# Score products of three groups in one run, sums of one or two key tiles behind them, in an attention and expert kernel

## The reference

```python
q = (layernorm(x) @ Wq.T).reshape(B, L, H, D) * D ** -0.5
k = (ctx @ Wk.T).reshape(B, -1, H, D)
v = (ctx @ Wv.T).reshape(B, -1, H, D)
scores = sigmoid(einsum('blhd,bshd->bhls', q, k))
x = x + einsum('bhls,bshd->blhd', scores, v).reshape(B, L, E) @ Wo.T
h = layernorm(x)
# 16 experts take 64 tokens of each batch by softmax gate, and one shared
# expert takes all: gelu(h Wg) * (h Wu) Wd, added to x
```

## Time and profile before

| | us |
|---|---|
| median of 3 runs | 1501.34 |
| lowest and highest | 1501.15, 1503.25 |
| the profiled execution's own time | 1503.28 |
| its span | 1501.4 |
| TensorE busy | 1412.4 (94%) |
| ScalarE busy | 888.2 (59%) |
| VectorE busy | 698.8 (47%) |
| weighted sums on TensorE, L1170, 3328 matmuls | 447.8 |
| scores on TensorE, L1154, 1664 matmuls | 316.8 |
| sigmoids on ScalarE, L608, 832 | 780.8 |

### The profile page before, as it was taken

The page is one execution under the profiler, slowest core; times in us unless marked ns, Lnnn a source line. Parts: engine busy times, 40 slices in busy tenths (PEclk is TensorE's granted clock), DMA queues, the critical chain, the costliest instruction groups (busy, mean ns, idle before and its releaser), DMA issues.

```text
span 1501.4 us, 22519 instructions
## 1 busy us (share of the span) xinstructions
PE 1412.4 (94%) x9046; PEld 786.8 (52%) x9046; DVE 698.8 (47%) x1369; ACT 888.2 (59%) x965; POOL 315.2 (21%) x203
## 2 busy tenths in 40 slices
PE   3888999999999999999999999998999999999996
PEld 2433344434434434444443443325888887778775
DVE  4334234225325314423522531224578987767764
ACT  0475877787787787788878779993211222222220
POOL 0000000000000000000000000020001588888885
PEclk9898999999999999999999999998999999999998
DMA  4573485396287467458639528613443545555543
GB/s 154 168 124 103 109 134 147 109 139 166 97 128 144 134 105 128 144 109 130 152 109 155 135 78 109 136 53 127 140 136 104 182 96 137 137 137 133 135 97 42
DMA packets 101144, 187.73 MB, mean 125 GB/s; under 512 B 17200, under 2 KB 51504, under 8 KB 101040
## 3 DMA queue, kind: packets, MB, share of 16 engines
q1 hardware_dynamic: 84192, 155.06, 44.2%
q0 software_dynamic: 16000, 29.91, 10.6%
q10 hardware_dynamic: 848, 1.31, 0.3%
HBM read 122.24 MB, written 64.00 MB: 124 GB/s over the span
## 4 chain that ended last, share of the span: by engine, by line
PE 76%; POOL 9%; DVE 5%; DMA 4%; issue 3%; ACT 2%; SPq 1%; POOLq 0%; DVEq 0%
PE acc L1170 25%; PE score L1154 17%; PE score L1210 11%; PE misc L1068 6%; PE misc L1081 6%; PE score L1225 4%; POOL gu_lo L532 3%; POOL out L564 3%; POOL d_lo L532 2%; PE misc L1104 2%; PE misc L1089 2%; ACT probs L608 2%; DMA key_scr<-key_parts 1%; PE misc L1113 1%; PE misc L1096 1%
## 5 line engine op out<-in xcount | busy, mean ns | idle before, releaser
L608 ACT ACTIVATE probs<-score 128x1024 f32<-128x1024 f32 (+1 forms) x832 | 780.8, 1048 | 205.8 <-PE score L1154 205.0
L1170 PE MATMUL acc<-probs,values 128*32 128x512 f32 (+1 forms) x3328 | 447.8, 610 | 5.7 <-ACT probs L608 3.1
L1154 PE MATMUL score<-queries,keys 48*128 48x512 f32 (+1 forms) x1664 | 316.8, 454 | 2.7 <-DMA keys<-key_scr 2.7
L617 ACT ACTIVATE gelu<-score 128x512 f32<-128x512 f32 x96 | 57.5, 599 | 346.3 <-PE score L1210 344.1
L1154 PEld LDWEIGHTS score<-queries,keys 48*128 48x128 f32 (+1 forms) x1664 | 127.3, 182 | 255.6 <-ACT probs L608 204.4
L510 POOL DMA_DIRECT2D ctx_raw<-ctx_t x32 | 23.4, 733 | 808.4 <-DVE ctx_lo L682 807.3
L1170 PEld LDWEIGHTS acc<-probs,values 128*32 128x32 f32 (+1 forms) x3328 | 66.4, 108 | 153.0 <-issue 131.4
L688 DVE CAST key_parts<-misc 128x512 fp32r<-128x512 f32 (+1 forms) x64 | 36.8, 576 | 213.2 <-PE misc L1068 198.7
L1210 PE MATMUL score<-tok_hi,gu_hi 128*128 128x512 f32 x384 | 121.4, 398 | 7.9 <-POOL gu_lo L532 7.9
L1210 PE MATMUL score<-tok_lo,gu_hi 128*128 128x512 f32 x384 | 119.7, 393 | 0.0
L1210 PE MATMUL score<-tok_hi,gu_lo 128*128 128x512 f32 x384 | 119.3, 392 | 0.0
(11 more groups left out here) (126 smaller groups left out, 1518.6 us busy)
## 6 DMA issues: line engine op xcount, KB each, us to landing
keys<-key_scr SPq DMA_DIRECT2D x180, 200.2 KB, 10.3
key_scr<-key_parts SPq DMA_DIRECT2D x48, 512.0 KB, 4.4
gu_raw<-w_gu SPq DMA_DIRECT2D x17, 1024.0 KB, 5.6
ctx_raw<-ctx_t POOLq DMA_DIRECT2D x24, 512.0 KB, 4.4
queries<-query_scr SPq DMA_DIRECT2D x180, 64.0 KB, 3.0
d_raw<-w_d SPq DMA_DIRECT2D x17, 512.0 KB, 6.7
query_scr<-query_parts SPq DMA_DIRECT2D x15, 512.0 KB, 2.9
xn<-x SPq DMA_DIRECT2D x8, 512.0 KB, 3.8
```

Source lines behind the costliest of these rows:

```text
L608: act.activation(probs[0:rows, n % RING, 2 * pair:2 * pair + 2, :], score[k % 3][0:rows, :, :], ACT.Sigmoid, scale=SCALE).then_inc(probs_d ...
L1154: mm = pe.matmul(score[k % 3][0:rows, g, :], keys[quarter % KEY_RING][of, pair, P * st:P * st + rows], queries[half][of, e, pair, :], star ...
L1170: mm = pe.matmul(acc[32 * c:32 * (c + 1), :], values[b % 2][0:rows, st, half, c, :], probs[0:rows, n % RING, c, :], start=(st == 0), stop= ...
```

## The change

The order on TensorE is no longer made by quads but by cycles, in a list (`PLAN`) that all engines follow. Cycle c begins with the scores of three groups, 3c to 3c + 2, that is one and a half quads. Then come the weighted sums of the quads both of whose groups are in earlier cycles and that are not summed yet: one quad in odd cycles, two in even ones. Then come the tasks whose quad (by the same table, `beside`) falls in the cycle. Where a cycle has two tasks, the first stands ahead of the sums; where a quarter ends in the cycle, the task stands behind that quarter's last sum. VectorE's and SyncE's steps follow the same plan. The arithmetic, the tiles, the three score tensors and the room for three quads in `probs` stay.

The diff, with SyncE's and VectorE's loops cut (they call the same steps as before, by cycle in place of quad):

```diff
@@ -24,12 +24,13 @@
 SCALE = HD ** -0.5
 
 
+
 QUARTERS = 4 * B
 QPB = 4 * NST
 QUADS = QPB * B
 GROUPS = 2 * NST
 RING = 3
-LAG = 2
+RUN = 3
 KEY_RING = 3
 
 
@@ -95,7 +96,31 @@
 
 
 BESIDE = [beside(b) for b in range(B)]
-ORDER = BEFORE + [BESIDE[b][q] for b in range(B) for q in sorted(BESIDE[b])]
+
+
+def cycle_of(b, q):
+    return 2 * (QPB * b + q) // RUN
+
+
+def quads_summed(c):
+
+    return range((RUN * c - RUN) // 2 if c else 0, min(QUADS, RUN * c // 2))
+
+
+
+PLAN = []
+for c in range(cycle_of(B, 0) + 2):
+    sums = [("S", n) for n in quads_summed(c)]
+    tasks = [BESIDE[b][q] for b in range(B) for q in sorted(BESIDE[b]) if cycle_of(b, q) == c]
+    last = [i for i, (_, n) in enumerate(sums) if n % NST == NST - 1]
+    if len(tasks) > 1:
+        steps = tasks[:1] + sums + tasks[1:]
+    elif last:
+        steps = sums[:last[0] + 1] + tasks + sums[last[0] + 1:]
+    else:
+        steps = sums + tasks
+    PLAN.append(steps)
+ORDER = BEFORE + [step for steps in PLAN for step in steps if step[0] != "S"]
 AFTER = [("O", B - 1, 0), ("O", B - 1, 1), ("N", B - 1, 0), ("N", B - 1, 1), ("G", B - 1)]
 ORDER += AFTER
 
...
@@ -405,38 +430,37 @@
                     write_keys(task)
             load_resid_a(0)
             load_x(1)
-            for b in range(B):
-                for q in range(QPB):
-                    if q == 0 and b:
+            for c, steps in enumerate(PLAN):
+                for b in range(1, B):
+                    if c == cycle_of(b, 0):
                         stack_queries(b, 1)
                         stack_keys(4 * b + 2)
-                    if q == NST and b:
+                    if c == cycle_of(b, NST):
                         stack_keys(4 * b + 3)
-                    task = BESIDE[b].get(q)
-                    if task is not None:
-                        if task[:3] == ("K", 0, 0):
-                            first_keys(task[3])
-                        elif task[0] == "K":
-                            write_keys(task)
-                        elif task[0] == "Q":
-                            write_queries(*task[1:])
-                            if task == ("Q", 0, 1):
-                                stack_queries(0, 1)
-                                stack_keys(2)
-                                stack_keys(3)
-                            elif task[2] == 0:
-                                stack_queries(task[1], 0)
-                        elif task[0] == "T" and task[2] == KC - 1 and task[1] + 1 < B:
-                            load_x(task[1] + 1)
-                        elif task == ("N", b - 1, 0):
-                            store_norm(b - 1)
-                        elif task == ("N", b - 1, 1):
-                            store_norm_t(b - 1)
-                        elif task == ("G", b - 1):
-                            load_resid_a(b)
-                        if task == ("K", b + 1, 1, NCH - 1):
-                            stack_keys(4 * b + 4)
-                            stack_keys(4 * b + 5)
+                for task in steps:
...
@@ -836,32 +860,32 @@
...
+            for c, steps in enumerate(PLAN):
+                for step in steps:
+                    if step[0] != "S":
+                        copy_out(step)
+                    elif step[1] % NST == NST - 1:
+                        acc_out(step[1] // NST)
...
@@ -1137,24 +1161,24 @@
                     mm = gate_product()
                 mm.then_inc(misc_full, 1)
 
-            def scores(n):
+            def scores(k):
+                n, pair = divmod(k, 2)
                 b, half, e, st = quad_of(n)
                 quarter, rows = n // NST, key_rows(st)
-                if quarter == 0 and st % (CHUNK // P) == 0:
-                    pe.wait_ge(first_keys_in[P * st // CHUNK], STACK_DMAS)
-                if quarter and st == 0:
-                    pe.wait_ge(keys_in[quarter % KEY_RING], keys_loaded(quarter))
-                if e == 0 and st == 0:
-                    pe.wait_ge(queries_in[half], 2 * STACK_DMAS * (b + 1))
-                for pair in range(2):
-                    k = 2 * n + pair
-                    wait_past(pe, probs_done, k - 2)
-                    for g in range(2):
-                        of = slice(ROWS * g, ROWS * g + STACK)
-                        mm = pe.matmul(score[k % 3][0:rows, g, :],
-                                       keys[quarter % KEY_RING][of, pair, P * st:P * st + rows],
-                                       queries[half][of, e, pair, :], start=True, stop=True)
-                    mm.then_inc(scores_done, 1)
+                if pair == 0:
+                    if quarter == 0 and st % (CHUNK // P) == 0:
+                        pe.wait_ge(first_keys_in[P * st // CHUNK], STACK_DMAS)
+                    if quarter and st == 0:
+                        pe.wait_ge(keys_in[quarter % KEY_RING], keys_loaded(quarter))
+                    if e == 0 and st == 0:
+                        pe.wait_ge(queries_in[half], 2 * STACK_DMAS * (b + 1))
+                wait_past(pe, probs_done, k - 2)
+                for g in range(2):
+                    of = slice(ROWS * g, ROWS * g + STACK)
+                    mm = pe.matmul(score[k % 3][0:rows, g, :],
+                                   keys[quarter % KEY_RING][of, pair, P * st:P * st + rows],
+                                   queries[half][of, e, pair, :], start=True, stop=True)
+                mm.then_inc(scores_done, 1)
 
             def weighted_sum(n):
                 b, half, e, st = quad_of(n)
@@ -1182,18 +1206,17 @@
             pe.wait_ge(w_split, 6)
             for task in BEFORE[4:]:
                 product(task)
-            for n in range(QUADS):
-                b, q = divmod(n, QPB)
-                scores(n)
-                if n >= LAG:
-                    weighted_sum(n - LAG)
-                if n == QPB:
+            for c, steps in enumerate(PLAN):
+                for k in range(RUN * c, min(RUN * c + RUN, 2 * QUADS)):
+                    scores(k)
+                if c == cycle_of(1, 0):
                     pe.wait_ge(w_split, 8)
                     pe.wait_ge(gate_split, 2)
-                if q in BESIDE[b]:
-                    product(BESIDE[b][q])
-            for n in range(QUADS - LAG, QUADS):
-                weighted_sum(n)
+                for step in steps:
+                    if step[0] == "S":
+                        weighted_sum(step[1])
+                    else:
+                        product(step)
             product(AFTER[0])
             product(AFTER[1])
```

More of the change, by code:

```diff
@@ new lines, in _ @@
+                for task in steps:
+                    if task[:3] == ("K", 0, 0):
+                        first_keys(task[3])
+                    elif task[0] == "K":
+                        write_keys(task)
+                        if task[2:] == (1, NCH - 1) and task[1]:
+                            stack_keys(4 * task[1])
+                            stack_keys(4 * task[1] + 1)
+                    elif task[0] == "Q":
+                        write_queries(*task[1:])
+                        if task == ("Q", 0, 1):
+                            stack_queries(0, 1)
+                            stack_keys(2)
+                            stack_keys(3)
+                        elif task[2] == 0:
+                            stack_queries(task[1], 0)
+                    elif task[0] == "T" and task[2] == KC - 1 and task[1] + 1 < B:
+                        load_x(task[1] + 1)
+                    elif task[0] == "N" and task[2] == 0:
+                        store_norm(task[1])
+                    elif task[0] == "N":
+                        store_norm_t(task[1])
+                    elif task[0] == "G":
+                        load_resid_a(task[1] + 1)
@@ L837, in _ @@
                 copy_out(task)
[L839 to L842, removed]
-                    if q in BESIDE[b]:
[L844 to L852, removed]
+            for c, steps in enumerate(PLAN):
[4 more added lines that the diff above has]
+                        acc_out(step[1] // NST)
+                if c == cycle_of(0, 11):
+                    split_weight(WO)
+                    dve.wait_ge(gate_in, 16)
+                    dve.tensor_copy(gate_hi[:], gate_raw[:]).then_inc(gate_split, 1)
+                    dve.wait_ge(gate_split, 1)
+                    dve.tensor_tensor(gate_lo[:], gate_raw[:], gate_hi[:].bitcast(F32), ALU.subtract
+                                      ).then_inc(gate_split, 1)
+                for b in range(B):
+                    if b and c == cycle_of(b, 7):
@@ L853, in _ @@
                         second_sums(b - 1)
-                    if b and q == 9:
+                    if b and c == cycle_of(b, 9):
                         norm_scale()
-                    if b and q == 11:
+                    if b and c == cycle_of(b, 11):
                         norm_apply(norm, resid, norm_ready)
-                    if b + 1 < B and q == (21 if b == 0 else 15):
```

(6 more changed lines are left out.)

## The result

The changed kernel takes 1557.26 us (median of 4 runs, 1554.38 to 1563.84) against 1502.3 (4 runs): a ratio of 1.0372, 95% interval 1.0337 to 1.0406. It is slower by 55 us, where 32 were forecast. In the text, a low-clock window is a stretch in which the granted clock is 0.50, 1.2 GHz instead of 2.4; in these traces it lasts 3.4 us or a multiple of that.

The account below looks back on a forecast made before the run. TensorE bounds batches 0 to 6, ScalarE batch 7. Middle batches +3.8 each (+23 for six), batch 0 +5, batch 7 +4: +32 us on the 1501.34 median, 1533 predicted; 8-in-10 range 1514 to 1554.

Parts of the forecast that it names:

- The sign: Whole kernel: the change makes it slower, chance 0.87; faster 0.09, same 0.04.
- the mechanism: Attention scores: with three banks, a run's third group waits for the previous run's third sigmoid, so nothing carries between cycles.
- rival D: Vector engine's norm work meets shorter gaps, idle TensorE may bring lower clock: 10 to 25 us more, 1543 to 1558; chance 0.20.
- What a longer run saves: TensorE: 0.10 us saved per run of three, 0.14 per second sum in a row; together 5.6 us a batch.
- Rival A: Score runs: the third group costs 0.335 as the second does, not 0.235; +12 us, 1545; chance 0.12.
- The stall: After empty one-sum cycles the third score group waits for ScalarE: 1.09 us each, 56 times in batches 1 to 6.
- so only 2.2 of 122.0 are waits: Middle batches before the change: 2.2 us of each batch's 122.0 are waits, subtracted because the new count replaces them.
- The vector engine: After a chunk's last V product, the copy and context split delay the next K product: 0.8 us, four times in six batches.
- Other copies fit in 1.90: VectorE's copies other than the context-split chain finish within 1.90 us, so they add no cost.
- Batch 7: ScalarE is the bound; a pair of cycles takes 5.75 against 5.49 us, 17 pairs x 0.25, +4 us.
- Batch 0: First batch: 7 stalls x 1.09 + 1.3 - 5.6 + 2 for keys, +5 us.
- The keys of batch 1: Last key product comes 11 groups ahead of first use, not 12; about 1 to 2 us more wait, once.

Follow-up runs that it names:

- pull: Changed kernel, where an odd one-sum cycle has no product and the next has, that product moved one cycle earlier; 1507.39 us, ratio 1.0018 to the kernel before.
- late: Changed kernel with the third score group, in cycles following an empty one-sum cycle, moved behind the first sum; 1533.49 us, ratio 1.0190 to the kernel before.
- half_after: Changed kernel with sigmoids over half of each head's columns (256 of 512), the rest of probs zero; 1475.34 us, ratio 0.9799 to the kernel before.
- quads7: Changed kernel with the old order, scores of one quad then one sum, from quad 366 on (batch 7); 1555.49 us, ratio 1.0317 to the kernel before.
- norm: Changed kernel with the vector engine's three layer-norm pieces moved from quads 15, 17, 19 to 12, 14, 16; 1555.08 us, ratio 1.0337 to the kernel before.
- gate_before: Kernel before with the gate product reduced to its high parts, 8 matmuls of 16 columns instead of 24; 1482.57 us, ratio 0.9871.
- gate_after: Changed kernel with the gate product reduced to its high parts, 8 matmuls instead of 24; 1533.02 us, ratio 1.0201 to the kernel before.

## Why the prediction was wrong

The sign, the mechanism and its place were right; the size was too small, and the time lies 3 us above the range. It lies in the band of rival D (1543 to 1558), which had a chance of 0.20 and named both things that the sum had too small or not at all, the vector engine's waits and the lower clock. By its steps:

- **What a longer run saves.** Right. Runs of three 0.90, two sums 1.85. Taking each run, sum and product at its undisturbed length (the most frequent one of its kind), batches 1 to 6 shrink from 717.9 to 686.4 us, 31.5 (to within 1 us); forecast 33.6. Rival A is out. TensorE: Matmul & The Clock Gate (the Trainium skill, section on row and column tiling) has a weight load overlap only matmuls of another row group, by which the run would last 1.00. The trace does not agree: the run lasts 0.90, and the load at 322.19 starts beside a matmul of its own row group.
- **The stall.** Right in place, count and size (55 of 1.09, forecast 56 of 1.09). With the smaller ones at transpositions the scores wait 63.5 us outside low-clock windows, forecast 66. pull, late and half_after confirm it from three sides.
- **The failing step: "so only 2.2 of 122.0 are waits".** That 2.2 a batch was subtracted from the forecast as waits that the new count replaces. Of the 14.1 us (732.0 less 717.9) that the steps of batches 1 to 6 lasted beyond their undisturbed lengths, about 6.7 were waits for ScalarE outside low-clock windows, and about 7.5 lay in steps that touch one of five such windows. After the change these were not gone but doubled, in the one profile of each kernel: nine windows, and 14.7 us. Why there are more of them is not settled: half_after, whose scores hardly wait for ScalarE, has 33 us of such windows too. The sum counted them out once and never in: about 15 us. It was named as a part of rival D ("longer idle stretches of TensorE may bring windows at the lower clock"), without a price in the sum.
- **The vector engine.** Forecast 3 us in six batches for one chain (the context split, 0.8 four times; found twice at 0.91, in front of the K products at 359.14 and 742.52). Measured, outside low windows: 3.8 in front of transpositions, 2.0 of K, 2.0 of Q products, together 7.8. The layer norm was left out ("Other copies fit in 1.90"), which holds when VectorE is free; in front of two transpositions and two Q products it was not. 5 us too little.
- **Batch 7.** Forecast +4 by 5.75 us a pair of cycles; measured +9.4. The pair was right: 5.73 by the double sums at 1037.04 and 1042.77, so 17 pairs give 4.1 (17 x 0.24, against 5.49). Of the 5.3 left, the sums slowed in two low-clock windows make 2.3 (the double sum at 970.67 took 3.29 instead of 1.85, the sum at 1022.72 1.87 instead of 1.00) and one quarter's end between two sums of a cycle 1.2; the rest is not accounted for. quads7 gives 7.4 back.
- **Batch 0.** Forecast +5, measured +1.5 with the later start. The keys of batch 1 are awaited 5.09 us instead of 2.66, 2.4 more, where "1 to 2 us more" was forecast. The stage had less of the lower clock than before, granted 0.96 against 0.93, some 9 us less of it; at 7.5 us lost for 17 us of it, as in batches 1 to 6 before, that gave back about 4 us (an estimate). That is luck: nothing in the forecast is about it.

Batches 1 to 6 in one line: -31.5 by shorter work, +56.8 at the scores (6.7 to 63.5), +7.8 at products, +7.2 by low-clock windows (7.5 to 14.7): 40.3, and 39.7 measured; the rest is within the reading of the undisturbed lengths.

What stays open: where the difference between runs (1554 to 1564) comes from. Each kernel has one profile, and the mean granted clock of the four runs (0.970, 0.965, 0.972, 0.972, the last for the slowest) does not follow their times. And rival D's two parts could not be separated in time (norm was inconclusive).

## What to carry to other kernels

- A ring of n buffers with runs of n hands over once per run and carries nothing from a rich cycle to a poor one. Ask of each cycle whether the other engine's part fits in, and count the cycles where it does not: an average over cycles says nothing. Here a switch saved 0.10 to 0.14 us, a handover missed cost 1.09.
- Before making runs longer, look which cycles are left without side work; moving a product by one cycle was worth 50 us here, more than the longer runs saved.
- Time beyond the undisturbed lengths is not all waits: read the clock before subtracting it.

## What the runs showed of the hardware

- Gate products of 24 matmuls with 16 moving columns, TensorE busy all along (2.90 of 2.90 us), preceded four of the five 3.4 us windows at 1.2 GHz (granted 0.50) in batches 1 to 6 of the kernel before; two of the six gate products there had none behind them. With 8 such matmuls instead of 24 (gate_before) none followed, and 20 us were gone, of which 7 x 1.8 = 12.5 are the matmuls themselves (2.78 to 0.99 us each).
- Idle time inside a run, 0.41 us in the rows above, preceded others (430.9, 816.6, 970.2 us in the changed kernel), at the same places in gate_after. It is not shown to be their cause: at the first two a short product comes between, and 52 of 55 such stalls have no window behind them. A sum that took 1.00 took 1.86 there.
- Behind a wait the weight load is not hidden: in the changed kernel it starts with the matmul at 248.55, and the next kind of work begins 0.42 us later (248.97), against 0.33 without a wait.
